# Depthwise convolution on tiles of 4 rows by 2 columns of 16 channels, in a fused two-convolution kernel

## Chip, core and metric

The kernel runs on one core of a Trainium2 chip. The metric is the device time of one execution in microseconds; before the change its median is 1674.36 us over 3 runs (1672.02 to 1674.77).

## What is computed

The input x is 8 images of 32 channels, 192 x 192, fp32. Two residual blocks follow each other:

```
x = x + conv3x3(bilinear_sample(gn(x), offsets = sigmoid(conv3x3(gn(x), w_off) + b_off)), w_dcn) + b_dcn
y = x
out = y + depthwise3x3(gn(y), taps)      # taps: relu(mean(gn(y)) @ w1 + b1) @ w2 + b2, per image and channel
```

`gn` is a group norm over pairs of channels and the whole image. Each offset lies in (-1, 1), so a sample needs only the pixel's direct neighbours. The depthwise taps depend on the mean of a whole image, so the second convolution of an image can't begin before its y is complete.

## The kernel before

Partitions hold 4 image rows (g) by 32 channels. A chunk is 16 rows: four such blocks, `NB = 4`, of 192 columns. An image has 12 chunks, the whole 96. All engines run the same loop over steps `i`, written out by hand for each engine, with semaphores between them:

- step i, PE: `offsets(i, 0)` and `offsets(i, 1)` (3x3 convolution to the x and y offsets, into PSUM banks `z`); then, interleaved in halves of two blocks, `depthwise(i - 17)` into the single bank `dw`, and `deform(i - 3)` into the two banks of `dc`. A convolution is banded: the contraction is 4 rows x 32 channels, the output 2 rows x 32 channels, and the two halves of the array (64 columns each) take the rows as they are (`sr`, `yr`) and a copy shifted by two rows (`sh`, `yh`). Three column taps accumulate. `conv` (line 333) emits them.
- ACT: `offset` (tanh out of `z`), `side` (masks `mu`, `mv`), `y_square(i - 4)`, `size`, the second `offset`, `side`, `size`, `finish(c, 0)`, `sides(i + 1)`, `finish(c, 1)`, with c = i - 17. In steps 1 to 8 of an image `x_sums` of the next image stands ahead of these. `finish` brings `dw` out to `ot`.
- DVE: `sample(i)` (lines 637 to 665: the bilinear sample by predicated copies and lerps), then `evacuate(i - 3)` (line 675: dc + bias + x into `yr`, with the sum for the statistics).
- SP, the queue of nearly all transfers: store of chunk i - 18, `s_shift(i - 1)`, `x_load(i + 2)`, a tile of the next image for the statistics, `residual(i - 3)` (x into `yr`), and `y_shift(i - 4)` (the shifted copy `yh`, right after y of a chunk is done). `yr` and `yh` are rings of 15 chunks.
- POOL: statistics, weights scaled by them, pads. At step 4 of the next image `y_norm` and `set_y_pads`, at step 5 `y_weights`. At step 0 `pivot` waits for the first statistics tile, and the pads of chunks 1 and 2 stand behind it.

For the last chunk of an image the second half of `deform` has an edge row of its own and goes as four tiles of 128x32 (line 376). For the last image `depthwise` uses the two banks of `dc`, which are free by then.

Of the kernel before, what the change touches and what calls it, by code (L numbers as in the profile page):

```python
# [7 lines left out]
F32 = mybir.dt.float32  # L8
# [5 lines left out]
P = 128  # L14
# [16 lines left out]
XS, SS, YS = 3, 3, 15  # L31
ABOVE, MID, BELOW = 0, 1, 2
BANK = 512
ROW = BANK // HALF
# [8 lines left out]
K_AVG, K_EYE, K_CEN = slice(0, P), slice(P, P + C), slice(P + C, P + C + 6)  # L43
# [4 lines left out]
C_XM, C_XV, C_OB, C_DB, C_YM, C_HID, C_TAP, C_WB = 0, 1, 2, 4, 5, 7, 8, 14  # L48
# [16 lines left out]
def r_dmas(n):  # L65
    return 3 if n % CHUNKS == CHUNKS - 1 else 1


def h_dmas(n):
    j = n % CHUNKS  # L70
    return 2 + (j > 0 and n % YS == 0) + (j == CHUNKS - 1)


def ring(n, slots, dmas):

    return 16 * sum(dmas(m) for m in range(n % slots, n + 1, slots))

# [20 lines left out]
def block_kernel(nc, x, planes, w_off, b_off, w_dcn, b_dcn, w1, b1, w2, b2, consts, out):  # L98
    with ExitStack() as ctx:
# [14 lines left out]
        yr = sb("yr", [P, YS * NB, WP])  # L114
        yh = sb("yh", [P, YS * NB, WP])
        ot = [sb(f"ot{s}", [P, NB, W]) for s in range(2)]
# [4 lines left out]
        wd = sb("wd", [P, 3, 2 * C])  # L121
        wds = [sb(f"wds{s}", [P, 3, 2 * C]) for s in range(2)]
        wy = [sb(f"wy{s}", [P, 3, 2 * C]) for s in range(2)]
        w1r = sb("w1r", [P, HID])
        w2r = sb("w2r", [HID, 6, P])
        b2r = sb("b2r", [P, 6])
        b1c = sb("b1c", [HID, 1])
        bo = sb("bo", [P, 2])
        bd = sb("bd", [P, 1])
        kc = sb("kc", [P, P + C + 6])  # L130
# [3 lines left out]
        ys1 = [sb(f"ys1{s}", [P, CHUNKS]) for s in range(2)]  # L134
# [12 lines left out]
        pooled = sb("pooled", [P, 1])  # L147
        hid = sb("hid", [HID, 1])
        tapr = sb("tapr", [P, 6])
        tap = sb("tap", [P, 6])  # L150
        ob = [sb(f"ob{s}", [P, 2]) for s in range(2)]
        db = [sb(f"db{s}", [P, 1]) for s in range(2)]
        wb = sb("wb", [P, 1])

        z = ctx.enter_context(nc.psum_tensor("z", [P, 2, 2, BANK], F32))
        dc = ctx.enter_context(nc.psum_tensor("dc", [P, NB, ROW], F32))
        dw = ctx.enter_context(nc.psum_tensor("dw", [P, HALF, ROW], F32))
# [10 lines left out]
        y_sh = [sem(f"y_sh{s}") for s in range(YS)]  # L168
# [30 lines left out]
        wd_ok = sem("wd_ok")  # L199
        wy_ok = sem("wy_ok")  # L200
# [11 lines left out]
        def first_tile(t, i):  # L212
            return t[:].rearrange("p k w -> p (k w)")[:, SW * i:SW * (i + 1)]
# [10 lines left out]
        def dw_bank(c, h):  # L224
            return dc[:, HALF * h:HALF * h + HALF, 0:W] if last_image(c) else dw[:, :, 0:W]

        @block.sync
        def _(sp):
# [23 lines left out]
            def residual(n):  # L252
                b, j = divmod(n, CHUNKS)
                k, done = y_at(n), r_in[n % YS]
                wait(sp, dw_mm, 2 * (n - YS + 1))
                line = P * j * NB + C
                m = NB - (j == CHUNKS - 1)
                sp.dma_start(yr[:, k:k + m, 1:W + 1], blocks_of(b, line, m)).then_inc(done, 16)
                if j == CHUNKS - 1:
                    line += P * m  # L260
                    sp.dma_start(yr[0:P - C, k + m, 1:W + 1], lines[b, line:line + P - C, :]).then_inc(done, 16)
                    sp.dma_start(yr[P - C:P, k + m, 1:W + 1], lines[b, 0:C, :]).then_inc(done, 16)
# [18 lines left out]
            def y_shift(n):  # L281
                b, j = divmod(n, CHUNKS)
                k, done = y_at(n), y_sh[n % YS]
                sp.wait_ge(y_done, n + 1)
                lo, hi = slice(0, P // 2), slice(P // 2, P)
                sp.dma_start(yh[lo, k:k + NB, 1:W + 1], yr[hi, k:k + NB, 1:W + 1]).then_inc(done, 16)
                if j == 0:
                    sp.dma_start(yh[hi, k:k + NB - 1, 1:W + 1], yr[lo, k + 1:k + NB, 1:W + 1]).then_inc(done, 16)
# [20 lines left out]
            for i in range(STEPS + 1):  # L309
# [11 lines left out]
                if 0 <= i - DCN_STEP - 1 < TOTAL:  # L321
                    y_shift(i - DCN_STEP - 1)
# [604 lines left out]
```

## Time and profile before

| | us |
|---|---|
| median of 3 runs | 1674.36 |
| profiled execution | 1668.98 |
| its span | 1667.2 |
| PE busy | 1557.6 (93%) |
| DVE busy | 1341.9 (80%) |
| ACT busy | 1050.6 (63%) |
| POOL busy | 304.9 (18%) |

The spans of a chain or timeline row are start and length in us from the start of the execution. A PE busy time is modelled and overlaps between the halves of the array, so what counts is the distance between starts. The granted clock of TensorE is 0.98 of full on the mean. The DMA engines are busy 65% with queue 1, most of it in packets below 2 KB.

### The profile page before, as it was taken

To read this page: it belongs to the slowest core of one execution; us is meant where nothing else is said; L and a number is where in the kernel's file an instruction comes from. 1 tells how busy PE (TensorE), PEld (TensorE's weight loads), DVE (VectorE), ACT (ScalarE), POOL (GpSimd) and SP (SyncE) were. 2 spreads that over 40 slices of the span, in tenths; PEclk is the share of its full clock that TensorE was granted. 3 is DMA by queue.
4 is the path that set the end of the run, shared out by engine and by line. 5 is a ranking of instruction groups with operands and counts; after the bars stand their busy time and mean duration, and the time that the engine had idled before them with its cause. 6 is when DMAs were issued, how large, how long until landed. Compare 5 with 4: busy or idle time off the path is not lost.

```text
span 1667.2 us, 25167 instructions
## 1 busy us (share of the span) xinstructions
PE 1557.6 (93%) x9856; PEld 730.4 (44%) x9856; DVE 1341.9 (80%) x1072; ACT 1050.6 (63%) x1546; POOL 304.9 (18%) x353
## 2 busy tenths in 40 slices
PE   3778777999999999999999999999999999999989
PEld 2334333444444444444444444444444445444334
DVE  3899979898888878898888988888788988889600
ACT  4767556766777567766677666775677665565422
POOL 3000313012230130303230122301402021400010
PEclk9899989999999999999999999999999999999999
DMA  6367657667686667767586676776586775666422
GB/s 227 114 193 199 164 149 206 193 190 194 181 229 193 180 176 213 201 192 194 167 230 196 185 198 177 223 192 188 166 224 192 196 189 158 184 168 170 118 86 105
DMA packets 296631, 304.28 MB, mean 183 GB/s; under 512 B 16288, under 2 KB 263616, under 8 KB 296512
## 3 DMA queue, kind: packets, MB, share of 16 engines
q1 hardware_dynamic: 296144, 302.05, 64.8%
q8 instruction: 78, 1.28, 0.3%
q0 software_dynamic: 368, 0.61, 0.1%
q14 instruction: 41, 0.34, 0.1%
HBM read 188.96 MB, written 37.75 MB: 136 GB/s over the span
## 4 chain that ended last, share of the span: by engine, by line
PE 81%; DVE 9%; issue 3%; ACT 3%; DMA 3%; POOL 1%; SPq 1%; DVEq 0%; POOLq 0%; ACTq 0%
PE z L333 38%; PE dc L333 21%; PE dw L333 19%; DMA st<-in_planes 2%; DVE nb L656 1%; DVE nb L651 1%; DVE nb L654 1%; DVE xv L644 1%; DVE nb L658 1%; DVE nb L660 1%; PE sm L406 1%; PE dc L376 1%; DVE nb L645 1%; DMA yr<-in_planes 1%; PE sm L437 1%
## 5 line engine op out<-in xcount | busy, mean ns | idle before, releaser
L333 PE MATMUL z<-xv,wos 128*64 128x384 f32 x4608 | 772.0, 491 | 30.7 <-issue 19.6
L333 PEld LDWEIGHTS z<-xv,wos 128*64 128x64 f32 x4608 | 347.3, 137 | 427.5 <-issue 406.3
L333 PE MATMUL dc<-sr,wds 128*64 128x384 f32 x1104 | 394.7, 496 | 31.6 <-DVE yr L675 31.6
L333 PE MATMUL dc<-sh,wds 128*64 128x384 f32 x1104 | 395.1, 496 | 0.0
L333 PE MATMUL dw<-yr,wy 128*64 128x384 f32 x1008 | 356.1, 489 | 1.2 <-ACT ot L523 1.1
L333 PE MATMUL dw<-yh,wy 128*64 128x384 f32 x1008 | 356.2, 489 | 0.0
L637 DVE COPY_PREDICATED nb<-mu,xv 128x2280 f32<-128x2280 uint16 x96 | 267.7, 2788 | 101.2 <-ACT mu L495 101.2
L333 PEld LDWEIGHTS dc<-sr,wds 128*64 128x64 f32 x1104 | 152.0, 139 | 221.8 <-issue 210.1
L488 ACT ACTIVATE du<-z,ob 128x768 f32<-128x768 f32 x96 | 86.2, 898 | 250.8 <-PE z L333 250.7
L509 ACT ACTIVATE nb<-xv 128x2292 f32<-128x2292 f32 x96 | 202.5, 2110 | 40.6 <-issue 40.3
L333 PEld LDWEIGHTS dw<-yr,wy 128*64 128x64 f32 x1008 | 135.7, 137 | 166.0 <-issue 148.4
L644 DVE COPY_PREDICATED xv<-mv,xv 128x768 f32<-128x768 uint16 x96 | 100.6, 1048 | 93.5 <-ACT mv L495 70.7
L654 DVE TENSOR_TENSOR nb<-nb,du 128x1536 f32<-128x1536 f32 x96 | 169.4, 1764 | 3.3
L656 DVE TENSOR_TENSOR nb<-nb,xv 128x1536 f32<-128x1536 f32 x96 | 169.0, 1761 | 3.3
L651 DVE TENSOR_TENSOR nb<-nb,xv 128x1536 f32<-128x1536 f32 x96 | 168.8, 1758 | 3.3
L333 PEld LDWEIGHTS dc<-sh,wds 128*64 128x64 f32 x1104 | 152.0, 139 | 5.5 <-issue 1.2
L523 ACT ACTIVATE ot<-dw,wb 128x384 f32<-128x384 f32 x168 | 96.2, 572 | 79.7 <-PE dw L333 79.3
L333 PEld LDWEIGHTS dw<-yh,wy 128*64 128x64 f32 x1008 | 135.7, 137 | 3.6 <-issue 0.6
L675 DVE SCALAR_TENSOR_TENSOR yr<-dc,db,yr 128x768 f32<-128x768 f32 x96 | 97.0, 1010 | 22.8 <-PE dc L333 15.9
L542 ACT ACTIVATE junk<-yr,nmx 128x768 bf16<-128x768 f32 x96 | 88.6, 923 | 40.5 <-DVE yr L675 40.5
L531 ACT ACTIVATE st<-st,npiv 128x1152 f32<-128x1152 f32 x56 | 70.1, 1252 | 68.1 <-DMA st<-in_planes 67.9
L488 ACT ACTIVATE dv<-z,ob 128x768 f32<-128x768 f32 x96 | 86.1, 897 | 30.0 <-PE z L333 29.8
(111 smaller groups left out, 1466.4 us busy)
## 6 DMA issues: line engine op xcount, KB each, us to landing
xv<-in_x SPq DMA_DIRECT2D x272, 384.0 KB, 4.7
out<-ot SPq DMA_DIRECT2D x96, 384.0 KB, 3.4
yh<-yr SPq DMA_DIRECT2D x179, 192.0 KB, 7.7
yr<-in_x SPq DMA_DIRECT2D x88, 384.0 KB, 8.2
st<-in_planes SPq DMA_DIRECT2D x56, 576.0 KB, 7.3
sh<-sr SPq DMA_DIRECT2D x160, 194.0 KB, 2.8
sh<-sr SPq DMA_DIRECT2D x32, 145.5 KB, 2.5
yr<-in_planes SPq DMA_DIRECT2D x8, 576.0 KB, 10.7
```

The costliest lines, as they stand in the source:

```text
L333: last = nc.tensor.matmul(acc[m], weights[:, kx, :], view[:, :, kx:kx + W], start=kx == 0, stop=kx == 2)
L488: nc.scalar.activation(d[:].rearrange("p (h k) w -> p h (k w)", h=2), z[:, i, :, 0:HALF * W], ACT.Tanh, bias=ob[b % 2][:, i:i + 1], scale= ...
L509: nc.scalar.activation(nb[s][:, :, :, 1:W], v[:, :, :, 1:W], ACT.Copy)
L523: nc.scalar.activation(ot[n % 2][:, HALF * h:HALF * h + HALF, :], dw_bank(n, h), ACT.Identity, bias=wb[:]).then_inc(o_done, 1)
L531: nc.scalar.activation(st[s][:], st[s][:], ACT.Identity, bias=npiv[:], accum_out=xs1[:, i:i + 1]).then_inc(centred, 1)
L542: nc.scalar.activation(junk[:].rearrange("p (k w) -> p k w", w=W), yr[:, k:k + NB, 1:W + 1], ACT.Square, bias=nmx[b % 2][:], accum_out=ys2 ...
L637: nc.vector.copy_predicated(q[:, :, :, 1:W - 1], m3[:, :, :, 1:W - 1], v[:, :, :, 3:W + 1]).then_inc(lerp, 1)
L644: nc.vector.copy_predicated(v[:, ABOVE, :, 1:W + 1], m1, v[:, BELOW, :, 1:W + 1]).then_inc(lerp, 1)
L651: nc.vector.tensor_tensor(two, two, own, ALU.subtract).then_inc(lerp, 1)
L654: nc.vector.tensor_tensor(two, two, u2, ALU.mult).then_inc(lerp, 1)
L656: nc.vector.tensor_tensor(two, two, own, ALU.add).then_inc(x_free, 1)
L675: nc.vector.scalar_tensor_tensor(out=y, in0=dc[:, :, 0:W], scalar=db[b % 2][:], in1=y, op0=ALU.add, op1=ALU.add, accum_out=ys1[b % 2][:, j ...
```

## The change

Depthwise convolution: the partitions of `yr` now hold 4 rows x 2 column parities x 16 channels; a block has two channel halves q of 96 column pairs each (`PAIRS`), with a pad column on both sides (`PW` = 98). The output of one pass is 2 rows x 2 parities x 16 channels, and two shifted reads (t) of the pairs cover the three column taps. A pass covers all four blocks of a chunk for one channel half: 4 x 97 = 388 columns (`OW` = 97), two passes per chunk, with other weights (`wy` of `Q x 2 x 64`, 8 tap vectors for 6).

Deformable convolution: its output must arrive in that layout, so each pass makes the 16 channels of one half q, split into four tiles of 32 output columns (rows as they are or shifted, times column parity). Each tile reads every second column of `sr` or `sh`. For an image's last chunk the moved tiles take three matmuls, with two sets of edge weights that POOL makes (`edge_weights`).

The residual x comes from a new array `xr`, laid out on the host, in one transfer per chunk. The evacuation is one DVE op per channel half. `yh` is a ring of 4 chunks, copied late: `y_shift(i - 15)` for most chunks, and for an image's first chunk `y_shift(i - 16)`, which waits until POOL has set the pads of y; a copy `yf` keeps the image's first block for its last. The edge rows come from a tile `ypad` by four POOL-queue transfers. The host undoes the layout.

```diff
-            def deform(n, h):
+            def deform(n, q):
...
+                wait(pe, y_done, Q * (n - 1) + q + 1)
                 weights = wds[b % 2]
...
+                whole, moved = sr[:, k:k + NB], sh[:, k:k + NB]
                 for kx in range(3):
+                    for r, view in enumerate((whole, moved)):
+                        for h in range(2):
+                            m = slice(C * (2 * r + h), C * (2 * r + h) + C)
+                            cols = slice(kx + h, kx + h + W - 1, 2)
+                            first, final = kx == 0, kx == 2
+                            if r == 0 or j < CHUNKS - 1:
+                                last = nc.tensor.matmul(dc[m, q, 0:NB * PAIRS], weights[:, kx, q], view[:, :, cols],
+                                                        start=first, stop=final)
+                                continue
+                            n3 = (NB - 1) * PAIRS
+                            nc.tensor.matmul(dc[m, q, 0:n3], weights[:, kx, q], view[:, 0:NB - 1, cols],
+                                             start=first, stop=False)
+
+                            nc.tensor.matmul(dc[m, q, n3:n3 + PAIRS], wde[:, 0, kx, q], view[:, NB - 1, cols],
+                                             start=False, stop=False)
+                            last = nc.tensor.matmul(dc[m, q, n3:n3 + PAIRS], wde[:, 1, kx, q],
+                                                    sh[:, SS * NB + b % 2, cols], start=False, stop=final)
                 last.then_inc(dcn_mm, 1)
...
+            def depthwise(n, q):
+                b, j = divmod(n, CHUNKS)
+                if q == 0:
+                    if j == 0:
+                        pe.wait_ge(wy_ok, b + 1)
+                    pe.wait_ge(y_sh[n % HS], ring(n, HS, h_dmas))
+                    if j == CHUNKS - 1:
+                        pe.wait_ge(e_in, 16 * EDGES * (b + 1))
...
-                    wait(pe, o_done, 2 * n + h)
-                conv(dw_bank(n, h), wy[b % 2], yr[:, k:k + HALF, :], yh[:, k:k + HALF, :]).then_inc(dw_mm, 1)
+                    wait(pe, o_done, Q * n + q)
+                acc, k, h = dw_bank(n, q), y_at(n), h_at(n)
+                for t in range(2):
+                    for m, view in zip(halves, (yr[:, k:k + NB, q], yh[:, h:h + NB, q])):
+                        last = nc.tensor.matmul(acc[m], wy[b % 2][:, q, t], view[:, :, t:t + OW],
+                                                start=t == 0, stop=t == 1)
+                last.then_inc(dw_mm, 1)
```

```diff
             def y_square(n):
...
-                act.wait_ge(y_done, n + 1)
+                act.wait_ge(y_done, Q * (n + 1))
...
             def evacuate(n):
...
+                for q in range(Q):
+                    y = yr[:, k:k + NB, q, 1:PAIRS + 1]
+                    dve.wait_ge(dcn_mm, Q * n + q + 1)
+                    nc.vector.scalar_tensor_tensor(
+                        out=y, in0=dc[:, q, 0:NB * PAIRS].rearrange("p (k w) -> p k w", w=PAIRS),
+                        scalar=db[b % 2][:, q:q + 1], in1=y, op0=ALU.add, op1=ALU.add,
+                        accum_out=ys1[b % 2][:, q, j:j + 1]).then_inc(y_done, 1)
```

```diff
             def y_shift(n):
...
-                sp.wait_ge(y_done, n + 1)
...
                 if j == 0:
+                    sp.wait_ge(y_row, y_rows(b + 1))
+                    wait(sp, e_in, EDGES * 16 * (b - 1))
+                    sp.dma_start(yf[hi, b % 2], yr[lo, k]).then_inc(f_in[b % 2], 16)
+                wait(sp, dw_mm, Q * (n - HS + 1))
+                sp.dma_start(yh[lo, h:h + NB], yr[hi, k:k + NB]).then_inc(done, 16)
...
                     residual(i - DCN_STEP)
-                if 0 <= i - DCN_STEP - 1 < TOTAL:
-                    y_shift(i - DCN_STEP - 1)
+                for n in (i - DW_STEP + 1, i - DW_STEP + 2):
+                    if 0 <= n < TOTAL and (n % CHUNKS == 0) == (n == i - DW_STEP + 1):
+                        y_shift(n)
...
+            def set_y_edges(b):
+                n = CHUNKS * b + CHUNKS - 1
+                k, h = y_at(n) + NB - 1, h_at(n) + NB - 1
                 pool.wait_ge(y_row, y_rows(b + 1))
...
+                pool.wait_ge(y_sh[n % HS], ring(n, HS, h_dmas))
+                for p0 in (P - 3 * CQ, P - CQ):
+                    pool.dma_start(yr[p0:p0 + CQ, k], ypad[p0:p0 + CQ]).then_inc(e_in, 16)
+                for p0 in (0, C):
+                    pool.dma_start(yh[p0:p0 + CQ, h], ypad[p0:p0 + CQ]).then_inc(e_in, 16)
```

## Rows read from the trace of the kernel before

**Rows 1.** The page, part 1: busy time, share and instructions of each engine.
```profile
PE 1557.6 (93%) x9856; PEld 730.4 (44%) x9856; DVE 1341.9 (80%) x1072; ACT 1050.6 (63%) x1546; POOL 304.9 (18%) x353
```

**Rows 2.** The chain that ended last, its longest pieces: start, length, what.
```profile
339.12 7.74 PE z L333 x48
354.60 7.74 PE z L333 x48
...
386.33 7.89 PE z L333 x48
403.73 7.79 PE z L333 x48
421.52 7.96 PE z L333 x48
...
597.50 7.79 PE z L333 x48
...
1615.58 48.21 PE dc L333 x288
```

**Rows 3.** Timeline of PE around an edge chunk: start, length, what, count.
```profile
839.48 0.48 PE L333 MATMUL dw<-yr,wy 128*64 128x384 f32 x1
...
839.92 0.52 PE L376 MATMUL dc<-sr,wds 128*32 128x384 f32 x2
...
841.56 0.49 PE L376 MATMUL dc<-sr,wds 128*32 128x384 f32 x2
...
842.00 7.96 PE L333 MATMUL z<-xv,wos 128*64 128x384 f32 x48
```

**Rows 4.** Timeline of DVE in a step of the first image; idle in brackets.
```profile
124.68 1.01 DVE L675 SCALAR_TENSOR_TENSOR yr<-dc,db,yr 128x768 f32<-128x768 f32 x1
...
125.62 2.81 DVE L637 COPY_PREDICATED nb<-mu,xv 128x2280 f32<-128x2280 uint16 x1
129.19 1.05 DVE L644 COPY_PREDICATED xv<-mv,xv 128x768 f32<-128x768 uint16 x1 [0.76 <-ACT mv L495]
...
140.46 2.77 DVE L637 COPY_PREDICATED nb<-mu,xv 128x2280 f32<-128x2280 uint16 x1
```

**Rows 5.** Timelines of PE, DVE and ACT in step 2 of an image.
```profile
826.25 7.94 PE L333 MATMUL z<-xv,wos 128*64 128x384 f32 x48
...
832.27 0.08 DVE L675 DVE_READ_ACCUMULATOR yr<-dc,db,yr 128x1 f32 x1
...
836.64 0.56 ACT L523 ACTIVATE ot<-dw,wb 128x384 f32<-128x384 f32 x1
```

**Rows 6.** Timelines of DVE, SP, POOL and PE from step 0 to 1.
```profile
795.25 0.96 DVE L665 TENSOR_TENSOR sr<-nb 128x768 f32<-128x768 f32 x1
...
799.30 0.50 SPq L250 DMA_DIRECT2D st<-in_planes  x1
...
806.74 0.23 POOL L705 TENSOR_SCALAR npiv<-st 128x1 f32<-128x1 f32 x1 [13.04 <-DMA st<-in_planes]
...
810.75 7.96 PE L333 MATMUL z<-xv,wos 128*64 128x384 f32 x48 [2.25 <-issue]
```

**Rows 7.** Groups by line and shape: busy us, mean ns of one, idle before.
```profile
L675 DVE SCALAR_TENSOR_TENSOR yr<-dc,db,yr 128x768 f32<-128x768 f32 x96 | 97.0, 1010 | 22.8 <-PE dc L333 15.9 <-PE dc L376 6.9
...
L437 PE MATMUL sm<-hid,w2r 64*128 64x1 f32 x96 | 12.0, 249 | 0.0
...
L684 DVE SCALAR_TENSOR_TENSOR st<-yr,npiv,zero 128x1152 f32<-128x1152 f32 x8 | 11.3, 1418 | 9.3 <-POOL npiv L705 7.0 <-DMA yr<-in_planes 1.7
```

**Rows 8.** The page, part 6: transfers, KB each, us from issue to landing.
```profile
yh<-yr SPq DMA_DIRECT2D x179, 192.0 KB, 7.7
...
sh<-sr SPq DMA_DIRECT2D x160, 194.0 KB, 2.8
```

**Rows 9.** Timelines of PE and POOL in step 4 of an image.
```profile
857.95 4.41 PE L333 MATMUL z<-xv,wos 128*64 128x384 f32 x26
...
864.03 3.38 POOL L806 TENSOR_SCALAR yr<-zero,mvy 128x72 f32<-128x72 f32 x2
```

More of the change, by code:

```diff
@@ L65, in r_dmas, with y_rows @@
 def r_dmas(n):
-    return 3 if n % CHUNKS == CHUNKS - 1 else 1
+    return 1
 def h_dmas(n):
-    j = n % CHUNKS
-    return 2 + (j > 0 and n % YS == 0) + (j == CHUNKS - 1)
+    return 3 if n % CHUNKS == CHUNKS - 1 or n % YS == YS - 1 else 2
 def ring(n, slots, dmas):
     return 16 * sum(dmas(m) for m in range(n % slots, n + 1, slots))
+EDGES = 4
+def y_rows(b):
+    return sum(2 + (CHUNKS * m % YS > (CHUNKS * m + CHUNKS - 1) % YS) for m in range(b))
 def pads_set(n):
@@ L253, in residual @@
                 b, j = divmod(n, CHUNKS)
[L254 to L262, printed above, removed]
+                k = y_at(n)
+                wait(sp, dw_mm, Q * (n - YS + 1))
+                if n >= YS:
+                    sp.wait_ge(y_sh[(n - YS) % HS], ring(n - YS, HS, h_dmas))
+                sp.dma_start(yr[:, k:k + NB], xr[b, j]).then_inc(r_in[n % YS], 16)
             def s_shift(n):
@@ L421, in x_biases @@
                 pe.wait_ge(wd_ok, b + 1)
-                biases("db", b, C_DB, (wds[b % 2],), nmx[b % 2][:])
+                small_turn("db", b)
+                for q in range(Q):
+                    for kx in range(3):
+                        for g in range(G):
+                            last = nc.tensor.matmul(sm[C * g:C * g + C, C_DB + q:C_DB + q + 1], wds[b % 2][:, kx, q],
+                                                    nmx[b % 2][:], start=kx == 0, stop=kx == 2)
+                last.then_inc(small, 1)
             def y_means(b):
@@ L442, in y_bias @@
                 pe.wait_ge(wy_ok, b + 1)
-                biases("wb", b, C_WB, (wy[b % 2],), my_neg[:])
+                small_turn("wb", b)
+                for q in range(Q):
+                    for t in range(2):
+                        for m in halves:
+                            last = nc.tensor.matmul(sm[m, C_WB + q:C_WB + q + 1], wy[b % 2][:, q, t], my_neg[:],
+                                                    start=t == 0, stop=t == 1)
+                last.then_inc(small, 1)
             pe.wait_ge(loaded, LOADED)
@@ L798, in set_y_pads @@
                 first, last = CHUNKS * b, CHUNKS * b + CHUNKS - 1
-                for n in range(first, last + 1):
-                    pool.wait_ge(y_sh[n % YS], ring(n, YS, h_dmas))
                 runs = [(y_at(first), y_at(last) + NB)]
```

275 lines of the change are left out of this document (150 added, 125 removed).

## Prediction

> **What bounds the kernel now.** I read the page first: TensorE (PE) is busy 93% of the span, DVE 80% [rows 1]. A share is only a mean, so I went to the chain of waits and looked for the start of each step, a step being one chunk of 16 image rows and its 48 offset matmuls. An undisturbed step is 15.48 us from start to start, and those 48 matmuls take 7.74, or 0.3225 us for each pair that runs side by side, one "slot" (24 slots) [rows 2]. One call is two instructions for each half of the array, so offsets take 24 slots, `deform` 12, `depthwise` 12: 48 x 0.3225 = 15.48. TensorE has no gap in such a step and is the bound.
>
> Two stretches are different. From step 11 of an image to step 1 of the next it takes 35.2 us, where two bare steps would be 31.0 [rows 2]. There the end of `sample` on DVE lets SP issue the first statistics tile; the tile lands 7.4 us after its issue, only then can POOL set pivot and pads, and PE, idle for 2.25 us, starts [rows 6]. From the start of DVE's last op of that sample to PE's start is 810.75 - 795.25 = 15.5 us: a chain of DVE, SP, DMA and POOL, without matmuls of the changed kinds. And in the first image no `depthwise` runs, PE has 11.6 us of work in a step, yet a step takes 14.84 [rows 4]. That shows the second limit. DVE ends an evacuation and starts the next copy at 125.62, but the copy after that waits 0.76 us for `mv` and starts at 129.19. ACT issues, in order, the square of the y just evacuated, size, offset, and `mv` (the row names `mv` as what ended the wait). So the end of one evacuation to the next `mv` copy is 3.57 us, from there to the end of the next evacuation 11.27: a loop of 14.84 us that PE can't shorten.
>
> **Part by part.**
> *Depthwise.* Two passes (channel half q) of two taps (t) in place of two passes of three: 8 slots of 388 columns, not 12 of 384: 8 x 0.3225 x 388/384 = 2.61 us for 3.87, a saving of 1.26 us per chunk.
>
> *Deform.* Still 12 slots, now each with four 128x32 tiles. The trace has this form in the last chunk of each image, line 376: sets of four start at 839.92 and 841.56, five slots apart, 0.328 each [rows 3]. So the work stays 3.87. What is paid is the change of tile shape: 839.48 to 839.92 and 841.56 to 842.00 are 0.44 each against 0.3225, 0.12 us a change [rows 3]. Before that is rare; now `deform` stands between 64-column work twice per step, four changes, +0.47. PE's step is 15.48 - 1.26 + 0.47 = 14.69.
>
> The Trainium skill speaks against this part: "TensorE: Matmul & The Clock Gate", Measured speedup vs the span model, gives three column tiles 2.38x and four row tiles 3.07x, not 3x and 4x. By that, four tiles would take 1.3 times as long as in the rows, `deform` would be 5.0 us and PE's step 15.9. The rows on line 376 disagree with it, and I take them.
>
> *Moving operand with step 2.* `deform` now reads every second fp32 column. No row has that. Lower bound: the contiguous slot, 0.3225; upper: the read takes twice as long, 0.645, as both halves of what lies under it are passed over. I take the lower, being the row of the same engine, type and tile count; the upper is a rival. By itself: "SBUF — State Buffer", Door 1: The DMA port swizzle, says that steps up to 4 fp32 elements are free; no run here shows it yet.
>
> *Evacuation in two.* One op of 768 is 1.01 us, one of 1152 is 1.42 [rows 7], so 1.06 ns per element and 0.19 us fixed. In the stream an evacuation takes 0.94 us from its start to the next op's [rows 4], of which 0.14 isn't elements. So a second op costs 0.14 to 0.28 us; I take 0.14, the slot. It lies inside the loop, since the square waits for both: 14.84 + 0.14 = 14.98 us (15.12 at the other end). This is now above PE's 14.69.
>
> *How they meet.* Let x be the end of the evacuation after the step's first matmul. ACT's first `finish` ends at 836.64 + 0.56 = 837.20, 4.93 us after the evacuation's end at 832.27, x being 6.02 there [rows 5]. The second `depthwise` half needs that bank. Before, PE comes to it at 11.6 after the step's start, 0.6 after `finish`; now at 7.74 + 1.30 + 1.94 + 0.24 = 11.2. So the next step starts no earlier than x + 5.1 + 3.5 = x + 8.6. With `mv` ready at 9.75 at the earliest (offsets 7.74, then ACT's offset and `mv`, and hops), the next x is max(9.75, x + 3.57) + 11.41 - step. This settles at a step of 14.98 after one or two at 14.69: PE gives up 0.3 us per step to the loop.
>
> *A steady image.* 193.8 us [rows 2] = 35.2 + ten steps of 158.6, which are 154.8 and 3.8 of small matmuls and shape changes. New in the ten: `taps` go from 12 to 16 instructions of 0.125 us each [rows 7], +0.5; the last chunk's `deform` gives the moved tiles 288 + 96 + 96 = 480 columns for 384, +0.97 us if nothing else happens, and +3.9 if the short pieces of the two tiles don't overlap; I take 1.8, nearer the plain column count, minus 0.24 for the shape changes that step had already. PE's ten steps are 146.9 + 3.8 + 0.5 + 1.6 = 152.8, and the loop adds 1.0 in the three or four steps that have no such extra: 153.8. Saving 4.8. The 35.2 stay: at its head is `sample`, not PE, and the shorter `depthwise` only makes the PE idle there longer; the larger bias pass (48 instructions for 12, about +1 us) hides in it.
>
> *Late copies of y.* `y_shift` moves from chunk n+4 to n+15 and gets in SP's queue a wait for `y_row` (first chunk of an image). Behind it stand its own copies, then the next step's store, s shift, x load, statistics tile. POOL begins the y pads 6.1 us into that step [rows 9]; with about 5 us for them, SP is released some 11 us in, 1 us after it gets there (it issues the statistics tile at 6.3 [rows 6] and three more transfers), and the next store isn't due before 14: nothing behind it is late. Copies landed 7.7 us after issue when queued behind x, 2.8 alone [rows 8]: done by 21 us, while the first `depthwise` needs them at 17 + 8 = 25. Cost 0, cover 4 us. The four edge DMAs on POOL's queue stand before `y_norm`, with a step to spare. The copies no longer write 768-byte rows but 3 KB runs, which can only help.
>
> **Sum**, on the profiled execution (span 1667.2, whole 1669.0). Five full images 5 x 4.8 = 24. Six steps of image 2 after `depthwise` begins: 3.6. The last image's twelve steps, without the 35.2 stretch's hiding: 4.7. First image and the four steps after: 17 x 0.14, -2.5. Five steps after the last offsets: three save 0.8, two 1.26 and lose some to the statistics chain, 4. Last twelve chunks: 48.21 us now [rows 2], `depthwise` alone, 4.0 each; PE would take 2.61, but a chunk's copies are now issued behind the store three chunks before: 2.61 + 0.7 for ACT + about 1.1 of issues + 2.8 landing [rows 8] = 7.2 for three, 2.4 each, and with the store in the same queue 3.0. I take 2.8: 34, saving 14. Total 24 + 3.6 + 4.7 - 2.5 + 4 + 14 = 48. The profiled execution would take 1621; the median of the runs is 5.4 above the profiled one, so **1626 us**.
>
> **Rivals.**
> A. *PE stays the bound, edge cheap*: the square's wait costs nothing and steps are 14.69. 0.3 x some 45 steps and 1 us per edge: 1606. Against it: the first image's steps at 14.84 with PE idle.
> B. *The loop and edges cost their upper bounds*: +0.14 x 90 = 13, edge +2.1 x 7 = 15, tail at 3.1 per chunk +4, of which half together: 1645.
> C. *The step-2 read is slow* (the slower side): each tenth on a `deform` slot is 0.39 us of PE per step, of which the first 0.3 only fills what the loop leaves idle. The 48 us of the sum, over some 82 steps, are gone at 0.59 us per step above 14.98, which is a slot 1.23 times as long: from there it decides. Doubled: 14.69 + 3.87 = 18.6 per step, 3.6 x 82 = 290 more and some in the first image: about 1930. For it: no row has such a read. Against it: four tiles run at full pace on contiguous columns.
> D. *Four tiles slow each other* when they run for a whole step, not for 12 slots: slots of 0.42, PE's step 15.85, 0.87 x 82 = 71 more: about 1697. Against it: the twelve slots of line 376 [rows 3], with no sign of a growing distance. The skill's packing figures above are this case.
> E. *The late copies don't make it*: the first `depthwise` of an image waits; each us over the 4 of cover is 7 us, and a PE idle of 3 us or more may halve the granted clock for some microseconds, as it did in the last steps: 1640 to 1690.
>
> **Chances.** Forecast with its small errors 0.62; A 0.12; B 0.12; C 0.07; D 0.03; E 0.04. A measurement tells 0.2% (3 us) from no change. The range reaches from A to B and a little beyond: 1605 to 1650. Faster: 0.62 + 0.12 + 0.12 = 0.86, with a part of E 0.87; same 0.02; slower 0.11, which is C, D and a little of E.
>
> **What would show it.** Right: `deform` sets of four start 0.32 apart; undisturbed steps of 15.0 us; PE waits for ACT's first `finish` by some tenths in them; DVE's `mv` copy still waits 0.5 to 0.8 for ACT; boundary stretch still 35; DVE's evacuation pair 1.08 from start to next op; the last twelve chunks in 32 to 36 us. Wrong: slots of `deform` over 0.35; a wait of PE for the y copies or for POOL's edge DMAs; statistics tiles that land later than 7.5 us and drag `mu`.

## The result, and the profile after

The changed kernel is slower: 1699.4 us, median of 4 runs (1696.91 to 1710.64), against 1673.19 of the kernel before in the same session (1671.93 to 1674.77). The ratio is 1.0169, with a 95% interval of 1.0122 to 1.0216. Timed again later (the last experiment) it was 1.0131, 1.0071 to 1.019. The forecast was 1626.

The page of the changed kernel, part 1, and of part 5 the rows of the two kinds of matmul that changed (busy us and mean ns of one; idle before and what ended it):

```profile
PE 1574.7 (93%) x12176; PEld 671.1 (40%) x12176; DVE 1356.8 (80%) x1264; ACT 1052.9 (62%) x1586; POOL 313.5 (18%) x381
...
L397 PE MATMUL dc<-sr,wds 128*32 128x384 f32 x2304 | 453.4, 525 | 25.7 <-DVE yr L739 25.6
...
L427 PE MATMUL dw<-yr,wy 128*64 128x388 f32 x672 | 258.1, 506 | 4.6 <-ACT ot L575 3.7
```

Against [rows 1]: TensorE has the same share of a span that is 31.7 us longer (1698.9 for 1667.2), and is busy 17 us more although `depthwise` lost a third of its passes. The chain of waits, its longest pieces:

```profile
330.82 7.89 PE z L357 x48
345.86 7.89 PE z L357 x48
360.92 7.89 PE z L357 x48
...
1639.10 6.92 PE sm L483 x32
1652.32 17.42 PE dc L427 x88
1669.81 5.64 DMA yh<-yr
1675.50 10.65 PE dc L427 x64
1686.15 3.88 issue
1690.03 5.45 PE dc L427 x16
```

An undisturbed step is 345.86 - 330.82 = 15.04 us, where [rows 2] had 15.48. So the main saving came. What ate it is seen when each step's length is taken from the starts of its 48 offset matmuls. The table gives the usual lengths in images 3 to 8; step 4 after the change is given for each image. Single steps differ: before, steps 3 and 4 of image 7 take 16.27 and 18.33; after, one step 0 takes 18.97; steps 0 and 1 of the last image are shorter, 15.51 and 15.48 before, 15.22 and 15.04 after.

| step of an image | before | after | forecast | 
|---|---|---|---|
| 0, 1, 11 | 17.97; 15.50 or 17.19; 17.29 | 17.97; 15.10 or 16.75; 17.30 | unchanged together |
| 2 (last chunk's `deform`) | 15.75 | **18.15** | 16.5 |
| 3, 5, 9, 10 | 15.95, 15.83, 15.89, 15.95 | 15.40, 15.51, 15.38, 15.35 | 0.8 less each |
| 4 (`hidden`, `taps`) | 17.22 | **20.39, 23.60, 21.90, 23.57, 23.53, 20.55** | 16.9 |
| 6, 7, 8 | 15.48 | 15.04 (8: up to 16.0) | 14.98 |

By stretches of the profiled execution, against the forecast for the same stretches (in us): to the first offsets of image 3, 408.9 for 402.5 forecast, +6.4 (step 4 of image 2 alone takes 26.4 for 19.2 before); from there to the last offsets 1173.3 for 1118.2, +55; to the last twelve chunks 70.1 for 61.1, +9; those chunks 43.2 for 34, +9. That is the whole of the 80 us between 1619 and 1699.

Step 4 of image 6 on TensorE (start, length, what, idle before), with POOL's operation that ends its wait:

```profile
1081.36 0.34 PE L476 MATMUL sm<-pooled,w1r 128*64 128x1 f32 x3 [1.22 <-POOL pooled L867]
...
1085.24 4.59 PE L483 MATMUL sm<-hid,w2r 64*128 64x1 f32 x32
1089.77 0.91 PE L427 MATMUL dw<-yr,wy 128*64 128x388 f32 x1
...
1090.47 0.85 PE L427 MATMUL dw<-yr,wy 128*64 128x388 f32 x1
...
1092.56 0.86 PE L397 MATMUL dc<-sr,wds 128*32 128x384 f32 x2
...
1094.95 0.51 PE L397 MATMUL dc<-sr,wds 128*32 128x384 f32 x2
```
```profile
1078.43 2.87 POOL L867 TENSOR_SCALAR pooled<-pooled,ry 128x2 f32<-128x2 f32 x1
```

`taps` is 32 instructions, one column each, two for each of the 16 vectors. Behind it the matmuls last 0.85 us instead of 0.5 and start 0.65 apart instead of 0.33, until 1094.95. The view by windows says what that is (the third number from the end of a row is the granted TensorE clock):

```profile
1081.30:1089.70 8.40, 8.35 (x68) 6.02 (x68) 7.57 (x6) 4.26 (x6) 3.15 (x4) 0.89 1.06 336
1089.80:1094.90 5.10, 5.10 (x25) 1.52 (x28) 1.55 (x2) 2.19 (x4) 0.00 (x0) 0.52 0.26 87
1095.70:1126.00 30.30, 30.30 (x244) 12.04 (x240) 23.65 (x23) 20.95 (x31) 3.18 (x6) 1.00 0.67 198
```

The clock fell to half of full speed, the 1.2 GHz level, and TensorE had been busy since 1081.36. The fall lies inside `taps`: a mean of 0.89 over the 8.40 us of the first window is 1.8 us at half clock, and `taps` takes 4.59 us here for 3.73 in image 3, where the clock stays up. The whole low stretch is 6.8 us, from 1087.9. In images 4, 6 and 7 it is as long and begins 2.3 to 2.7 us after the first of the 32 instructions; in images 5 and 8 it is 3.4 us and begins 4.5 and 4.8 us after it, behind `taps`; in image 3 there is none. The account of a step 4: 17.22 before, -0.44 as in a regular step, +2.23 for `taps` (3.73 us without a clock drop during it, 1.50 before), +1.4 for POOL (TensorE begins `hidden` 9.2 us into the step, not 7.8): 20.4, as in image 3. Images 4 to 7 are 1.5 or 3.2 longer, by how long the low clock lasted. In image 8 TensorE doesn't wait for POOL, and the low clock takes up what that saves: 20.55.

A regular step on TensorE, which starts at 1126.42; some rows of its blocks:

```profile
1134.21 0.49 PE L427 MATMUL dw<-yr,wy 128*64 128x388 f32 x1
...
1135.62 0.54 PE L397 MATMUL dc<-sr,wds 128*32 128x384 f32 x2
...
1135.98 0.51 PE L397 MATMUL dc<-sr,wds 128*32 128x384 f32 x2
...
1137.35 0.52 PE L397 MATMUL dc<-sr,wds 128*32 128x384 f32 x2
...
1137.81 0.54 PE L427 MATMUL dw<-yr,wy 128*64 128x388 f32 x1
```

`deform` starts a set every (1137.35 - 1135.98) / 4 = 0.343 us, against 0.328 for line 376 in [rows 3]. From `dw` to `dc` it is 0.43, from `dc` to `dw` 0.46: 0.11 and 0.12 more than the slot, as in [rows 3]. Nowhere in the step does TensorE wait.

### The profile page after: what moved, and what is told of

The parts are those of the page before. It is cut to its first block, busy times and chain, and to the rows that moved or that the text cites. A ratio compares the mean times of both kernels' runs of the same rounds, so it can differ in the third digit from the quotient of the medians.

```text
span 1698.9 us, 30216 instructions
## 1 busy us (share of the span) xinstructions
PE 1574.7 (93%) x12176; PEld 671.1 (40%) x12176; DVE 1356.8 (80%) x1264; ACT 1052.9 (62%) x1586; POOL 313.5 (18%) x381
## 4 chain that ended last, share of the span: by engine, by line
PE 54%; DVE 19%; ACT 11%; issue 6%; DMA 5%; POOL 3%; SPq 2%; DVEq 0%; ACTq 0%; POOLq 0%
PE z L357 25%; PE dc L397 13%; PE dw L427 9%; DMA st<-in_planes 4%; DVE nb L718 3%; DVE nb L713 3%; DVE nb L716 3%; PE sm L483 2%; ACT dv L540 2%; PE dc L427 2%; DVE xv L706 2%; DVE nb L720 2%; DVE nb L722 2%; ACT mv L547 2%; DVE nb L707 2%
## 5 line engine op out<-in xcount | busy, mean ns | idle before, releaser
L397 PE MATMUL dc<-sr,wds 128*32 128x384 f32 x2304 | 453.4, 525 | 25.7 <-DVE yr L739 25.6
L397 PE MATMUL dc<-sh,wds 128*32 128x384 f32 x2112 | 411.8, 527 | 0.0
L427 PE MATMUL dw<-yr,wy 128*64 128x388 f32 x672 | 258.1, 506 | 4.6 <-ACT ot L575 3.7
L427 PE MATMUL dw<-yh,wy 128*64 128x388 f32 x672 | 258.2, 506 | 0.0
L397 PEld LDWEIGHTS dc<-sr,wds 128*32 128x32 f32 x2304 | 123.4, 111 | 296.4 <-issue 294.8
L575 ACT ACTIVATE ot<-dw,wb 128x388 f32<-128x388 f32 x168 | 96.7, 576 | 68.8 <-PE dw L427 68.4
L739 DVE SCALAR_TENSOR_TENSOR yr<-dc,db,yr 128x384 f32<-128x384 f32 x192 | 110.6, 613 | 21.5 <-PE dc L406 9.1
L727 DVE TENSOR_TENSOR sr<-nb 128x768 f32<-128x768 f32 x96 | 93.1, 969 | 32.4 <-PE dc L397 20.8
L583 ACT ACTIVATE st<-st,npiv 128x1152 f32<-128x1152 f32 x56 | 70.1, 1253 | 75.4 <-DMA st<-in_planes 75.4
L397 PEld LDWEIGHTS dc<-sh,wds 128*32 128x32 f32 x2112 | 113.2, 112 | 0.8 <-issue 0.8
L707 DVE COPY_PREDICATED nb<-mv,nb 128x768 f32<-128x768 uint16 x96 | 100.4, 1046 | 0.0
```

What stands on the lines that cost most here:

```text
L397: last = nc.tensor.matmul(dc[m, q, 0:NB * PAIRS], weights[:, kx, q], view[:, :, cols], start=first, stop=final)
L427: last = nc.tensor.matmul(acc[m], wy[b % 2][:, q, t], view[:, :, t:t + OW], start=t == 0, stop=t == 1)
L707: nc.vector.copy_predicated(q[:, ABOVE], m1, q[:, BELOW]).then_inc(lerp, 1)
L739: nc.vector.scalar_tensor_tensor(out=y, in0=dc[:, q, 0:NB * PAIRS].rearrange("p (k w) -> p k w", w=PAIRS), scalar=db[b % 2][:, q:q + 1], i ...
```

## The experiments

The theories, with the letters that the expectations use. T: the 32 tiny matmuls of `taps` cost their own time and bring the granted clock down for the matmuls behind them. U: the clock falls because TensorE waits for POOL's `pooled` before `hidden`. V: the step-2 read of `deform`, or its four tiles, cost something in every step. Beside these stand the last chunk's short pieces, the four changes of tile shape, and the late copies.

### `taps` in one matmul

```diff
-                for t in range(TAPS):
-                    last = nc.tensor.matmul(sm[:, C_TAP + t:C_TAP + t + 1], w2r[:, t, :], hid[:], ...)
+                last = nc.tensor.matmul(sm[:, C_TAP:C_TAP + TAPS], w2r[:, 0, :], hid[:].to_broadcast([HID, TAPS]), ...)
```

> The changed kernel, but one matmul call (2 instructions) fills all 16 tap columns with the first tap vector; 15 of 16 calls are left out, so the taps are wrong. Theory T (the loss sits in step 4 of each image, in the tap matmuls and in the slow clock that follows them): 30 instructions x 0.14 us = 4.2 us less per image, and dw/dc behind them back at 0.325 to 0.34 a slot in place of 0.645; step 4 falls from 20.4 to 23.6 us to about 17 to 18, the total from 1699 to 1650 to 1660. Rival U (the slow clock comes from PE's wait for POOL ahead of them, the taps cost only their instructions): step 4 keeps slots of 0.645 in the images that had them, total 1665 to 1670. Rival V (every step is slower because of four tiles with step-2 reads): step 4 falls by 4 us at most, the total stays above 1665.

Measured: 1654.93 us (1653.13 to 1656.67), ratio to the kernel before 0.9905 (0.988 to 0.9931). Step 4 is 17.1 us in images 3 to 7 and 15.6 in image 8, where TensorE doesn't wait for POOL. The other steps are as in the changed kernel, but for steps 0, 1 and 8, which scatter there too. TensorE in the same place as above:

```profile
1067.47 0.34 PE L476 MATMUL sm<-pooled,w1r 128*64 128x1 f32 x3 [1.23 <-POOL pooled L866]
...
1071.41 0.39 PE L482 MATMUL sm<-hid,w2r 64*128 64x16 f32 x2
1071.73 0.54 PE L427 MATMUL dw<-yr,wy 128*64 128x388 f32 x1
```

The wait for POOL is as long as before, and the clock stays at 1.00 through step 4 of images 3 to 8. So 30 of the 32 instructions cost 44 us of the 1699. Their own time is 8 x (3.66 - 0.32) = 27 of it, from the first of them to the next matmul; the remaining 17 go with the clock. With `taps` this short the change is a gain of 1%, but about half of that, 8 x (1.43 - 0.32) = 9 us, is tap work that the kernel before does and this one leaves out. As the cause of these clock drops U falls.

### The kernel before, with sixteen tap vectors

```diff
                 for t in range(TAPS):
                     last = nc.tensor.matmul(sm[:, C_TAP + t:C_TAP + t + 1], w2r[:, t, :], hid[:], ...)
+                for t in range(10):
+                    last = nc.tensor.matmul(sm[:, 100 + t:101 + t], w2r[:, t % 6, :], hid[:], ...)
```

> The kernel before with ten more tap calls (20 instructions) into unused columns of the same bank; output unchanged. T: 20 x 0.13 = 2.7 us per image for the instructions, and the granted clock falls behind them in some images, 1 to 3 us more: 1674 + 8 x 4 to 5.5 = 1705 to 1718. U: only the instructions, 8 x 2.7 = 22, 1696, and all deform and depthwise slots stay at 0.3225. V: the same as U.

Measured: 1705.05 us (1700.32 to 1706.18), ratio 1.0197 (1.0164 to 1.023). Step 4 goes from 17.22 to 21.15, 23.89, 19.45, 21.14, 21.15 and 21.10 in images 3 to 8, and from 19.2 to 27.3 in image 2; the others stay, but for single steps of the kinds that scatter. In image 5, with 19.45, the clock stays up; in the other five it falls. TensorE and the clock in one of them:

```profile
1086.02 1.50 PE L437 MATMUL sm<-hid,w2r 64*128 64x1 f32 x12
1087.38 2.37 PE L440 MATMUL sm<-hid,w2r 64*128 64x1 f32 x20
1089.68 0.75 PE L333 MATMUL dw<-yr,wy 128*64 128x384 f32 x1
...
1090.22 0.85 PE L333 MATMUL dw<-yr,wy 128*64 128x384 f32 x1
```
```profile
1081.90:1089.60 7.70, 7.70 (x60) 5.79 (x57) 6.58 (x6) 5.22 (x7) 4.37 (x3) 1.00 1.02 295
1089.70:1093.30 3.60, 3.60 (x13) 1.39 (x14) 3.53 (x3) 0.00 (x0) 0.00 (x0) 0.53 0.23 54
```

TensorE never idles here, and nothing else of the change is in the kernel. Twenty more instructions of one column make the same drop and cost 32 us, 8 x 2.23 = 18 of it their own time. T holds: the effect is shown from both sides. Whether the number of the tiny matmuls or the time that they fill decides, these runs don't separate.

### `deform` with neighbouring columns

```diff
-                            cols = slice(kx + h, kx + h + W - 1, 2)
+                            cols = slice(kx + h, kx + h + PAIRS)
```

> The changed kernel, but deform reads 96 neighbouring columns in place of every second one (wrong columns, same sizes and weights). T: slots of deform go from 0.343 to 0.328 us, as on line 376 of the kernel before; PE's step to about 14.85, but the loop evacuation - square - mv copy holds it at 14.95 to 15.0: undisturbed steps lose under 0.1 us, the total 3 to 8 us. V: slots fall to 0.3225 and steps to 14.7, total 20 us or more less. If nothing moves, the 0.343 belong to four tiles that run for long, not to the step.

This kernel reads other columns than the reference wants. Measured: 1688.83 us (1681.63 to 1698.94), ratio 1.0113 (1.0062 to 1.0163). The unchanged kernel's own runs lie between 1684 and 1711 (the last experiment), so here, and in the experiments with 1683 to 1690 below, the total alone proves little; the lengths of steps decide. The first and the last of four sets of `deform`:

```profile
1136.17 0.50 PE L397 MATMUL dc<-sr,wds 128*32 128x384 f32 x2
...
1137.15 0.49 PE L397 MATMUL dc<-sr,wds 128*32 128x384 f32 x2
```

(1137.15 - 1136.17) / 3 = 0.327 us: the slot of [rows 3]. The step-2 read costs 0.016 a slot, 5%, or 0.19 per step; steps are 14.82, below the 14.95 that I expected the loop to allow. Four tiles over twelve slots in every step hardly slow each other (0.327 for 0.3225). So V is right in kind and small, and rivals C (twice as long) and D (0.42) are out.

### Short pieces of the last chunk, tiles alternating

```diff
                 for kx in range(3):
-                    for r, view in enumerate((whole, moved)):
-                        for h in range(2):
+                    for part in range(3 if edge else 1):
+                        for r, view in enumerate((whole, moved)):
+                            if r == 0 and part > 0:
+                                continue
+                            for h in range(2):
...
+                                elif part == 0:
                                     nc.tensor.matmul(dc[m, q, 0:n3], ...)
+                                elif part == 1:
                                     nc.tensor.matmul(dc[m, q, n3:n3 + PAIRS], wde[:, 0, kx, q], ...)
+                                else:
                                     last = nc.tensor.matmul(dc[m, q, n3:n3 + PAIRS], wde[:, 1, kx, q], ...)
```

> The changed kernel with the last chunk's calls in another order: the 288-column pieces of the two moved tiles first, then their first 96, then their second 96, so that pieces of two tiles can run side by side. Output unchanged. T: step 2 of an image falls from 18.15 to 16.3 to 16.9 us, the total by 7 x 1.3 to 1.8 plus about 2 in the last image: 1699 to 1685 to 1688. Rival (the short pieces are bound by their weight loads, 0.11 us each, not by the order): step 2 stays within 0.3 us of 18.15.

Measured: 1683.26 us (1680.78 to 1687.45), ratio 1.0078 (1.0049 to 1.0106). Step 2 falls from 18.15 to 16.13, a little more than expected, and the other steps stay within the changed kernel's scatter. The rival, weight loads, would have left it at 18.15. First the changed kernel, where a tile's two short pieces follow each other, then this one:

```profile
1048.92 0.25 PE L404 MATMUL dc<-sh,wde 128*32 128x96 f32 x1
...
1049.10 0.33 PE L406 MATMUL dc<-sh,wde 128*32 128x96 f32 x2
1049.22 0.42 PE L401 MATMUL dc<-sh,wds 128*32 128x288 f32 x1
...
1050.03 0.25 PE L404 MATMUL dc<-sh,wde 128*32 128x96 f32 x1
```
```profile
1045.16 0.35 PE L408 MATMUL dc<-sh,wde 128*32 128x96 f32 x4
...
1045.35 0.35 PE L411 MATMUL dc<-sh,wde 128*32 128x96 f32 x4
1045.52 0.44 PE L405 MATMUL dc<-sh,wds 128*32 128x288 f32 x2
```

Tile after tile, the pattern repeats every 1050.03 - 1048.92 = 1.11 us, and one half of `deform` takes 3.76 us, from 1047.82 to `depthwise` at 1051.58. Alternating, it takes 2.74, from 1044.62 to 1047.36. A tile's second piece, issued ahead of the other tile's first, seems to keep that one waiting. The order costs 2.0 us per image; what is left over a regular step of 15.04 is 1.1.

### Sixteen tap vectors in eight matmuls

```diff
-        w2r = sb("w2r", [HID, TAPS, P])
+        w2r = sb("w2r", [2 * HID, TAPS // 2, P])
-        hid = sb("hid", [HID, 1])
+        hid = sb("hid", [2 * HID, 2])
-                for t in range(TAPS):
+                for t in range(TAPS // 2):
```

Two vectors are stacked over 128 rows; the hidden values stand in the first column for the upper half and in the second for the lower, with zeros beside them.

> The changed kernel with the 16 tap vectors in 8 calls (16 instructions in place of 32): two vectors stacked over 128 rows, against the hidden vector in a 128x2 block form. Output unchanged. T: 16 x 0.14 = 2.3 us less per image, and with so short a run of tiny matmuls (1.5 us of them did no harm in the kernel before, 2.7 more did) the slots behind stay at 0.34: step 4 at 18.8 to 19.5 us, total 1699 - 8 x 2.7 = 1672 to 1680. U (the wait for POOL makes the slow clock): step 4 at 18.5 to 21, total about 1680 to 1685.

Measured: 1670.81 us (1665.01 to 1676.34), ratio 0.9988 (0.9971 to 1.0005): no slower than the kernel before, and 1 us below the expected range. Step 4 is 18.9 in images 3 to 7 and 17.6 in image 8:

```profile
1073.03 1.95 PE L483 MATMUL sm<-hid,w2r 128*128 128x2 f32 x16
1074.90 0.54 PE L427 MATMUL dw<-yr,wy 128*64 128x388 f32 x1
```

Sixteen instructions, all the work kept, and no slot of 0.65 behind them in images 3 to 8.

### The two halves of `deform` next to each other

```diff
                     depthwise(c, 0)
                     deform(d, 0)
+                    deform(d, 1)
                     taps(b - 1)
                     depthwise(c, 1)
-                    deform(d, 1)
```

> The changed kernel with both halves of deform next to each other and the second half of depthwise behind them: two changes of tile shape per step, not four. Output unchanged. T: PE's step 15.04 - 2 x 0.12 = 14.80, the loop through the square allows 14.82: undisturbed steps of 14.82 to 14.85, 0.2 us less in some 70 steps: total 1699 - 12 to 16. Rival: ACT's second finish comes 2.2 us later, pushes the statistics tile and mu of the next step, and steps 1 to 8 of an image gain nothing: total within 4 us of 1699.

Measured: 1690.41 us (1688.81 to 1694.08), ratio 1.0117 (1.0095 to 1.0138). The total falls between what T and the rival expected. Regular steps come down from 15.04 to between 14.75 and 14.83, two shape changes at 0.12 and a little more, but steps 0 and 1 of an image go up, to 19.0 and up to 17.5, and step 5 to between 16.2 and 16.8. What those steps wait for stays open.

### Copies of y one step earlier

```diff
-                for n in (i - DW_STEP + 1, i - DW_STEP + 2):
-                    if 0 <= n < TOTAL and (n % CHUNKS == 0) == (n == i - DW_STEP + 1):
+                for lead in (1, 2, 3):
+                    n = i - DW_STEP + lead
+                    if 0 <= n < TOTAL and min(n % CHUNKS, 2) + 1 == lead:
```

> The changed kernel with y_shift one step earlier for the chunks 2 to 11 of an image (the ring of 4 allows it). Output unchanged. T: in the last twelve chunks PE's stall of 2.6 us for a copy goes, and of the 6 us it waits for POOL's edge transfers before the last chunk about 2.6 go too; the middle doesn't move, since no depthwise there waits for a copy: total 3 to 6 us less. Rival (the copies also lie in the way of x and statistics tiles in the middle): boundary stretches of 35.2 or undisturbed steps move by more than 0.2 us.

Measured: 1686.43 us (1681.92 to 1691.35), ratio 1.0086 (1.006 to 1.0112). The steps with offsets keep their lengths, so the late copies cost nothing there, as forecast. After the last offsets it takes 110.1 us for 116.7, but that alone shows nothing: the unchanged kernel took 109.7 when it was timed again, with 12 us less at the low clock there. The last twelve chunks show it: 36.8 us, for 43.3 and 39.9 in the two traces of the changed kernel. In its last chunks one sees on ACT, whose line 575 is `finish`, and on POOL:

```profile
1677.07 0.59 ACT L575 ACTIVATE ot<-dc,wb 128x388 f32<-128x388 f32 x1 [2.62 <-PE dc L427]
1678.38 0.59 ACT L575 ACTIVATE ot<-dc,wb 128x388 f32<-128x388 f32 x1 [0.72 <-PE dc L427]
...
1692.92 0.59 ACT L575 ACTIVATE ot<-dc,wb 128x388 f32<-128x388 f32 x1 [6.13 <-PE dc L427]
```
```profile
1686.64 1.10 POOL L889 DMA_DIRECT2D yr<-ypad  x2 [35.39 <-DMA yh<-yf]
```

A half chunk takes 1.31 us with TensorE alone setting the pace. The two long waits are for the copies (1.9 us over the usual 0.72) and, before the last chunk, for POOL's edge copies, which it issues only at 1686.64 (5.4 us over). The earlier copies take the first away and shorten the second: TensorE's idle before the last chunk is 1.55 us for 3.88 (3.76 when timed again). Behind the 3.88 the last chunk runs at half clock, which is 2.6 of the 6.7 us lost there; behind the 1.55 it doesn't.

### All of these together, and the square of y moved

```diff
+    the edits of the last four experiments, and on ACT:
-                if 0 <= e < TOTAL:
-                    y_square(e)
-                ...
                 if c >= 0:
                     finish(c, 0)
+                if 0 <= e < TOTAL:
+                    y_square(e)
+                ...
```

> The changed kernel with the pairs of edge pieces (as e4), stacked taps, adjacent deform halves, earlier copies, and ACT's y_square moved behind the first finish, out of the way of mv. Output unchanged. T: undisturbed steps at PE's 14.80; step 2 at 15.9, step 4 at 18.8 to 19.5, last twelve chunks 38: 1699 - 16 (edges) - 24 (taps) - 15 (shape changes) - 5 (copies) = 1639, range 1630 to 1650, below the kernel before by 2%. If the loop through the square doesn't matter, e8 equals the sum of e4 to e7 without it. Rival: the gains don't add, since the boundary stretch takes them back; total above 1655.

Measured: 1636.89 us (1633.14 to 1637.79), ratio 0.9785 (0.9766 to 0.9803). This keeps all of the reference's work, beats both kernels and lies 2 us from the 1639 expected.

### The same without the moved square

> e8 without the move of y_square: ACT has it ahead of size, offset and mv again. T: the loop evacuation - square - mv holds undisturbed steps at 14.82 where PE would take 14.75; that is 0.07 in some 60 steps, and in the first image, where PE has no depthwise, steps return from the sampling's own 14.2 or so to 14.8: 13 steps x 0.5. Total 8 to 12 us above e8, 1645 to 1649. Rival (the square's place is worth nothing): within 3 us of e8, 1634 to 1640.

Measured: 1652.32 us (1649.64 to 1656.76), ratio 0.988 (0.985 to 0.9911). The move is worth 15 us here (the two were timed in different sessions), more than expected and not where I had it. Regular steps are between 14.75 and 14.83 in both. The first image is 5.5 us shorter with it (step 4 of image 2 starts at 267.5 for 273.0), and step 4 of images 3 to 7 is 18.7 to 18.9 with it and 20.8 (once 22.8) without, where TensorE waits longer for POOL and the clock falls. In image 8 it is the other way round, 18.5 with it and 17.5 without. First without the move, then with it, each with TensorE's row before `depthwise` and the window behind it:

```profile
1067.37 0.62 PE L482 MATMUL sm<-pooled,w1r 128*128 128x1 f32 x4 [1.74 <-POOL pooled L876]
...
1067.90:1070.70 2.80, 2.80 (x9) 0.77 (x9) 2.77 (x3) 0.91 (x3) 2.42 (x2) 0.50 1.12 353
```
```profile
1051.37 0.61 PE L482 MATMUL sm<-pooled,w1r 128*128 128x1 f32 x4 [1.37 <-POOL pooled L876]
...
1051.90:1054.40 2.50, 2.50 (x21) 0.89 (x24) 2.47 (x3) 1.98 (x5) 2.47 (x2) 1.00 1.08 341
```

So U isn't wrong in kind: in the kernel without the move the drop comes before `taps`, behind an idle of 1.72 to 2.23 us, in five of six images. It didn't come before `taps` behind idles of 1.06 to 1.37 in the kernel with the move and in the one with `taps` in one matmul, nor behind 1.67 to 1.69 in the one with adjacent halves.

### The changed kernel with only the square moved, and the kernel before with it

> The changed kernel; on ACT the square of y and the two small reads that go with it stand behind the first finish. If the loop evacuation, square, size, offset, mv bounds the regular steps (15.04 measured, TensorE's own sum with slots of 0.343 in deform is 14.87), these steps come down to 14.85 to 14.95, the first image's by 0.4 each as between the last two kernels (267.5 against 273.0 us at its 16th step), and step 4 by about 2: 0.15 x 40 + 6 + 2 x 7 = 26 less than the changed kernel, about 1669. If TensorE bounds them at 15.04 (slots longer than I take them), only the first image's 6 us come: about 1688.

> The kernel before with the same move of the square on ACT. If TensorE bounds its steps (48 slots of 0.3225 = 15.48) and ACT's order only the first image, regular steps stay at 15.48, the first image's eleven steps lose 0.4 each: 4 to 6 us less than the kernel before, 1667 to 1669. If the loop matters in its steps too, 1655 or less.

Measured: 1689.94 us (1678.73 to 1693.46), ratio 1.0104 (1.0063 to 1.0145), for the changed kernel; 1664.47 (1659.3 to 1672.96), ratio 0.9958 (0.9936 to 0.998), for the kernel before. In both the regular steps don't move, 15.04 and 15.48, and step 4 of image 2 starts 5 us earlier (268.7 for 273.7, and 268.1 for 273.0). For both kernels that is the outcome that I had tied to TensorE as the bound. So TensorE bounds the regular steps of both kernels, and ACT's order bounds only the first image. There the wait of 0.76 us for `mv` in [rows 4] is gone (DVE of the kernel before with the move):

```profile
124.23 2.81 DVE L637 COPY_PREDICATED nb<-mu,xv 128x2280 f32<-128x2280 uint16 x1
127.14 1.05 DVE L644 COPY_PREDICATED xv<-mv,xv 128x768 f32<-128x768 uint16 x1
```

The move is a gain of its own, 0.4% in the kernel before. Measured against that (1664.47), the combined kernel's 1636.89 is 1.7% less; the two were timed in different sessions, beside the kernel before at 1670.68 and about 1673.

### The changed kernel again

> The changed kernel as it is, beside e9 on one chip, to see how far its time scatters from run to run: 1697 to 1711 so far, with 2 to 4 us for each image whose step 4 falls into the slow clock. Every theory expects 1690 to 1710.

Measured: 1694.17 us (1683.56 to 1701.05), ratio 1.0131 (1.0071 to 1.019). In its trace steps 2, 3, 5 to 7 and 9 to 11 of images 3 to 8 have the lengths of the first one to 0.15 us. Step 4 is 21.99, 20.38, 23.63, 21.94, 23.67, 19.00; in images 4 and 8 the clock stays up. Steps 0, 1 and 8 scatter too. The trace is 11.7 us shorter than the first one: 3 of that are in step 4 of these images, 7 behind the last offsets, where the clock is low for 20 us and not for 33. So much of the scatter of this kernel between runs, 17 us, goes with how often and how long the clock falls.

## Why the prediction was wrong

**The price of `taps`: the step that failed.** I wrote "from 12 to 16 instructions of 0.125 us each, +0.5". There are sixteen vectors now, which is 32 instructions. That was a misreading: 12 instructions in [rows 7] are six vectors, and the loop in the diff runs sixteen times. The twenty instructions more than before cost 2.2 us per image, 18 in all. A part nearly as large no count would have given: during or behind 32 such instructions the granted clock falls to its lower level, for up to 3.2 us per image more, some 12 to 18 in all. (The first experiment is 39 to 44 us faster than the two timings of the changed kernel, and 27 of that is the time of 30 instructions.) At the forecast's own price for `taps`, 16 x 0.125 = 2.0 us per image where the first experiment has 0.32, the change would come to 1655 + 13 = 1668: of the 73 us between forecast and result this step is 31, the largest single part. The other 42 are in the next paragraphs; without them too the forecast would have been missed.

**The cover of `hidden`.** I hadn't priced the statistics chain ahead of it. In the kernel before POOL mostly had `pooled` ready 5.5 to 5.7 us into step 4, with TensorE arriving at 7.8, and DVE's long copy began at 6.0. In the changed kernel the chain's last op begins at 6.26 (the row at 1078.43 above), with DVE's copy, and lasts 2.87 us. Without DVE at work it takes 0.31, in the last chunks:

```profile
1636.23 0.31 POOL L867 TENSOR_SCALAR pooled<-pooled,ry 128x2 f32<-128x2 f32 x1
```

TensorE waits 1.2 us for it in images 3 to 7, and 6.6 in step 4 of image 2 instead of 4.2. The kernel before was close to this: in image 7 its op on `pooled` begins at 1253.70, with DVE's copy at 1253.61, and takes 2.69 us where it otherwise takes 0.19; TensorE waits 0.89 there, and step 4 is 18.33. The order decides: in image 8 of the changed kernel the op begins 0.29 us ahead of the copy and takes 0.31.

**The last chunk of an image.** Taken as 1.8, "nearer the plain column count"; measured 18.15 - 15.04 = 3.1 over a regular step. The upper bound of 3.9 was the nearer one, and the alternating order shows that two of the three are the order of issue. The step was forecast at 16.5: 1.65 us times 8, 13 in all.

**A regular step: the right number for the wrong reason.** TensorE's step was forecast at 14.69 and the loop over ACT at 14.98, which was to bind. Measured 15.04, near the latter, but it is TensorE: 7.79 + 1.41 + 2.19 + 1.45 + 2.20, block by block in the timeline from 1126.42 to 1141.46, with no wait. The difference to 14.69 is 12 x (0.343 - 0.3225) = 0.25 in the slots of `deform`, and 0.10 over the block ends. Of the 0.25, 0.19 is the step-2 read; the rest stood in [rows 3], whose 0.328 I had entered as 0.3225. The loop was real in the first image alone. Two mistakes cancelled, and that the number held was luck. They didn't cancel in steps 3, 5, 9 and 10, where I had TensorE bind: they save 0.55, 0.32, 0.51 and 0.60 us instead of 0.8, which is 1.2 per image. The third experiment shows it: with neighbouring columns, steps are 14.82, below what the loop was said to allow, and the square's move changes no regular step.

**Step-2 read.** I took the lower bound; it costs 5% (0.343 for 0.327). "SBUF — State Buffer", Door 1: The DMA port swizzle, of the Trainium skill, has steps up to 4 fp32 elements free; the measured 5% says nearly, not quite. The packing factor that I took from the Trainium skill, "TensorE: Matmul & The Clock Gate", Measured speedup vs the span model, 3.07x for four row tiles, would have made four tiles 1.3 times as long (that page has no figure for four column tiles); neither the third experiment's 0.327 nor 0.343 agrees with it.

**What held.** The shape change at 0.12 us. The stretch from step 11 to the next step 1 is 35.3 us in both kernels. DVE's pair of evacuations takes the forecast 1.08 us to the next op's start (1077.33 to 1078.41). Step 1 itself has two lengths, 1.7 us apart, in both kernels, and that is the clock: the longer ones are those with a stretch of 3.4 us at 0.50. In the kernel before they follow an idle of 2.25 us, less than the 3 us of rival E. The late copies of y cost nothing while offsets run. The step-2 and four-tile rivals, 0.10 together, were rightly small.

**The last twelve chunks.** Forecast 34, measured 43.2: twelve times 2.61 is 31.3, so the pace was even better than my 2.8. Added are 3.2 at the start, where the first matmuls follow `taps`, a POOL chain and a wait and run at half speed; 1.9 for copies; and 5.4 plus 1.3 before and in the last chunk, whose edge copies I had let pass with "a step to spare" and which here have none. The 9 us ahead of them are mostly `taps` again: 6.92 in the chain for 32 instructions, 0.22 each at the lower clock, where [rows 7] has 0.125. With one tap matmul this stretch is 62.1 us for 69.9.

**The chances.** Slower had 0.11, on C, D and a little of E; none of them happened as told (the late copies cost 1.9 us, once, behind the last offsets). None of my rivals had the granted clock fall without TensorE idling.

## What to carry to other kernels

Count the instructions of the small steps too, in calls times the instructions of a call, and look at the granted clock during and behind a run of one-column matmuls: stacking such vectors over unused rows halved their time and took away the drop. Where column tiles get pieces of unequal length, order them so that the tiles alternate. When a step is bound by the sum on one engine and a rival loop comes within 2% of it, a measured length doesn't tell which of the two binds; move something that only one of them contains.

## What was not expected of the hardware

- During or just behind 32 fp32 matmuls of one column (3.7 us without any idle time) the granted clock falls to 0.50 for 3.4 or 6.8 us, beginning 2.1 to 4.9 us after the first of them: in 5 and 4 of images 3 to 8 in the two traces of the changed kernel, in 5 of them in the kernel before with sixteen vectors, where TensorE doesn't idle ahead of them in four of the five. In the same images it stays at 1.00 behind 16 instructions of two columns (1.95 us) and behind 12 of one (1.50 us).
- A POOL operation on 128x2 elements took 0.31 us alone and 2.87 when it began together with DVE's predicated copy of 2.8 us; they ended within 0.15 us of each other. In the kernel before one on 128x1 took 2.69 for 0.19 in the same way. Begun 0.29 us ahead of the copy it took 0.31.
- A fp32 moving operand read with step 2 makes a slot of 384 columns 0.343 us for 0.327.
- A change between tiles of 64 and of 32 columns costs 0.11 to 0.12 us each way.
